# Fusion attention with each head's scores from its own 64 rows of the array, and keys without a masked product

## The reference, cut to what matters

```python
def _L0_attn_ref(x, Wq, bq, Wk, bk, Wv, bv, Wo, bo):
    # DIM 64, HEADS 4, HEAD_DIM 16, SCALE 0.25; x: (64, 205, 64)
    q = heads(x @ Wq.T + bq)
    k = heads(x @ Wk.T + bk)
    v = heads(x @ Wv.T + bv)
    attn = softmax(einsum('bhnd,bhmd->bhnm', q, k) * SCALE, axis=-1)
    out = einsum('bhnm,bhmd->bhnd', attn, v)
    out = out.transpose(0, 2, 1, 3).reshape(B, N, C)
    out = out.astype(bfloat16).astype(float32)
    return out @ Wo.T + bo

h = concatenate([image_branch(x), text_branch(x_txt)], axis=1)
h = h + _L0_attn_ref(_layernorm(h), ...)
h = h + _L0_ffn_ref(_layernorm(h), ...)
```

## Time and profile before

| what | value |
|---|---|
| median of 3 runs | 2437.77 us |
| lowest and highest run | 2432.27 and 2446.25 us |
| span of the profiled execution, first to last instruction | 2473.5 us |
| busy share of PE, PEld, DVE, ACT, POOL | 89%, 74%, 72%, 60%, 48% |
| stretch of fusion_attention | 1515.0 to 2061.5 us |
| mean granted clock of TensorE, whole span | 0.901 |
| DMA, whole span | 20.58 MB, mean 8 GB/s |

### The profile page before, as it was taken

How to read it: one execution, slowest core, us unless ns; L and a number is a source line. 1 busy time by engine, 2 the same in 40 slices (tenths; PEclk the granted TensorE clock), 3 DMA queues, 4 the chain that set the end, 5 groups by cost and what they waited for, 6 DMA issues and landing times. The chain is left out here.

```text
span 2473.5 us, 61351 instructions
## 1 busy us (share of the span) xinstructions
PE 2190.0 (89%) x19889; PEld 1822.7 (74%) x19889; DVE 1791.1 (72%) x5716; ACT 1489.8 (60%) x3226; POOL 1196.2 (48%) x1518
## 2 busy tenths in 40 slices
PE   6999999858999999999999934898888985999998
PEld 6999999746888888888888833676666764666665
DVE  5655555355888888888888845757877574888888
ACT  2222222105888888888888844656666565666663
POOL 3433333204777777777777644323433233344332
PEclk8999999957999999999999965858997576999999
DMA  2000022000000000000000000000000000000000
GB/s 87 14 20 13 13 51 43 1 1 1 2 2 3 2 3 2 2 2 2 2 2 3 2 1 1 0 0 0 0 0 0 0 0 1 8 10 8 8 10 11
DMA packets 39663, 20.58 MB, mean 8 GB/s; under 512 B 29508, under 2 KB 38852, under 8 KB 39366
## 3 DMA queue, kind: packets, MB, share of 16 engines
q1 hardware_dynamic: 39466, 18.00, 3.0%
HBM read 14.63 MB, written 3.36 MB: 7 GB/s over the span
## 5 line engine op out<-in xcount | busy, mean ns | idle before, releaser
L439 PE MATMUL im_c<-im_a_hi,im_w 128*128 128x256 f32 (+2 forms) x1920 | 427.9, 317 | 13.6 <-POOL im_a_lo L349 13.6
L439 PEld LDWEIGHTS im_c<-im_a_hi,im_w 128*128 128x128 f32 x1920 | 321.2, 191 | 30.5 <-POOL im_a_lo L349 13.8
L439 PE MATMUL im_c<-im_a_lo,im_w 128*128 128x256 f32 (+2 forms) x960 | 303.3, 316 | 0.0
L1041 POOL TENSOR_TENSOR tx_KB<-tx_KF,tx_head_rows 128x1248 fp32r<-128x1248 f32 x128 | 289.9, 2265 | 24.3 <-PE tx_scores_t L1326 15.5
L343 POOL TENSOR_TENSOR im_rstd<-im_var_eps,im_power 128x4 f32<-128x4 f32 x64 | 68.6, 1072 | 286.5 <-DVE im_var_eps L278 286.5
L902 DVE TENSOR_REDUCE tx_mpad<-tx_scores 77x8 fp32r<-77x616 f32 x256 | 202.1, 789 | 2.8 <-PE tx_maxT L1314 1.9
L1172 ACT ACTIVATE tx_PT<-tx_scores_t 77x624 f32<-77x624 f32 x256 | 175.8, 687 | 24.9 <-PE tx_scores_t L1326 18.3
L439 PEld LDWEIGHTS im_c<-im_a_lo,im_w 128*128 128x128 f32 x960 | 182.8, 190 | 8.3
L1326 PE MATMUL tx_scores_t<-tx_QP,tx_KB 128*77 128x78 f32 x2048 | 186.5, 241 | 0.0
L272 DVE BATCH_NORM_STATS2 im_stats<-im_h 128x6 f32<-128x128 f32 (+1 forms) x192 | 47.6, 302 | 190.6 <-ACT im_h L384 111.0
L1848 ACT ACTIVATE at_PT<-at_scores_t 128x824 f32<-128x824 f32 (+1 forms) x128 | 109.5, 855 | 120.9 <-PE at_scores_t L1921 120.9
(11 more groups left out here) (308 smaller groups left out, 6314.1 us busy)
## 6 DMA issues: line engine op xcount, KB each, us to landing
im_x<-x SPq DMA_DIRECT2D x16, 384.0 KB, 3.3
out<-h_img SPq DMA_DIRECT2D x32, 64.0 KB
tx_toks<-x_txt SPq DMA_DIRECT2D x1, 1925.0 KB
im_raw<-L_tok_conv_w SPq DMA_DIRECT2D x1, 1280.0 KB, 8.6
out<-h_txt SPq DMA_DIRECT2D x32, 38.5 KB
im_raw<-L_tok_conv_w SPq DMA_DIRECT2D x1, 960.0 KB, 4.8
im_raw<-L_tok_conv_w SPq DMA_DIRECT2D x1, 640.0 KB, 5.9
tx_raw_W<-L_txt_W SPq DMA_DIRECT2D x2, 256.0 KB, 7.1
```

Source lines behind the costliest of these rows:

```text
L439: last = pe.matmul(acc[:, :, d0:d1], w[c][:, slot, part], img[:, b0_:b1_, d0 + shift:d1 + shift, kj:kj + J], start=opens, stop=closes)
L1041: pool.tensor_tensor(KB[:, q % 2, t], KF[:, t].bitcast(F32).unsqueeze(1).broadcast_to([P, HPT, QW]), head_rows[:].unsqueeze(2).broadcast_t ...
```

## The change

The product with `head_rows` and with it `KB`, `head_rows` and the semaphore `k_split` are gone. `score` and `score_t` read the 64 rows of one head from `QF`, `KF` and `QP`, and so use 64 rows of the array at a time; head 0 lies on rows 0 to 63 and head 1 on rows 64 to 127. `score` has four matmuls of 206 columns for a tile instead of two of 412. The banks of `scores` and `scores_t` now belong to the head's place j instead of the tensor t, so that neighbouring matmuls write to different banks, and `find_max`, `exp` and `weigh` address them and `PT` in that order. `KF` gets a second buffer; the cut of the keys waits for the transposed scores of two samples before instead of for `k_split`.

```diff
-        lo_rows, head_rows = sb("lo_rows", [P, 2]), sb("head_rows", [P, A_HPT])
+        lo_rows = sb("lo_rows", [P, 2])
...
-        KF = sb("KF", [P, A_TENSORS, SEQP], F32R)
+        KF = sb("KF", [P, 2, A_TENSORS, SEQP], F32R)
         QF = sb("QF", [P, 2, A_TENSORS, SEQP], F32R)
-        KB = sb("KB", [P, 2, A_TENSORS, A_HPT, SEQP], F32R)
         QP = sb("QP", [P, 2, A_TENSORS, SEQP], F32R)
         mpad = sb("mpad", [P, 2, A_TENSORS, P], F32R)
-        PT = sb("PT", [P, 2, A_TENSORS, A_HPT * SEQP])
+        PT = sb("PT", [P, 2, A_HPT, A_TENSORS * SEQP])
...
-                        pool.memset(head_rows[rows, j:j + 1], 1.0).then_inc(indexed, 1)
-                        pool.wait_ge(indexed, 2 * j + 1)
                         pool.iota(row_index[rows], pattern=[[0, 1]], base=0, channel_multiplier=1).then_inc(indexed, 1)
-                        pool.wait_ge(indexed, 2 * j + 2)
...
-                    dst = QF[:, par, t] if is_q else KF[:, t]
+                    dst = QF[:, par, t] if is_q else KF[:, par, t]
                     dve.wait_ge(lo_part, m * 4 + (i + 1))
-                    if i == 0 and due(m * 2):
-                        dve.wait_ge(k_split, m * 2)
+                    if i == 0 and due(m * 2 - 2):
+                        dve.wait_ge(scored_t, m * 2 - 2)
...
-                    if live(n + 2):
-
-                        m = n + 2
-                        if due(m * 2 - 2):
-                            pool.wait_ge(scored_t, m * 2 - 2)
-                        for t in range(A_TENSORS):
-                            pool.wait_ge(qk_cut, m * 4 + (t + 1))
-                            pool.tensor_tensor(KB[:, par, t],
-                                               KF[:, t].bitcast(F32).unsqueeze(1).broadcast_to([P, A_HPT, SEQP]),
-                                               head_rows[:].unsqueeze(2).broadcast_to([P, A_HPT, SEQP]), ALU.mult)\
-                                .then_inc(k_split, 1)
...
-                        pe.wait_ge(k_split, m * 2 + 2)
                         pe.wait_ge(qk_cut, m * 4 + 4)
                     if due(m * 2 + tile):
                         pe.wait_ge(max_set, m * 2 + tile)
                     for t in range(A_TENSORS):
-                        last = pe.matmul(scores[0:n, t, 0:A_HPT * SEQP], QF[:, par, t, at:at + n],
-                                         KB[:, par, t].rearrange("p j s -> p (j s)"), start=True, stop=True)
+                        for j in range(A_HPT):
+                            head = slice(j * A_GROUP, (j + 1) * A_GROUP)
+                            last = pe.matmul(scores[0:n, j, t * SEQP:(t + 1) * SEQP], QF[head, par, t, at:at + n],
+                                             KF[head, par, t], start=True, stop=True)
...
-                            last = pe.matmul(scores_t[0:n, t, j * SEQP:(j + 1) * SEQP], KB[:, par, t, j, at:at + n],
-                                             QP[:, par, t], start=True, stop=True)
+                            head = slice(j * A_GROUP, (j + 1) * A_GROUP)
+                            last = pe.matmul(scores_t[0:n, j, t * SEQP:(t + 1) * SEQP], KF[head, par, t, at:at + n],
+                                             QP[head, par, t], start=True, stop=True)
...
-                             PT[0:kn, keys, t, j * SEQP:(j + 1) * SEQP],
+                             PT[0:kn, keys, j, t * SEQP:(t + 1) * SEQP],
```

More of the change, by code:

```diff
@@ L1654, in _ @@
                     pool.memset(oT[:].bitcast(F32), 1.0).then_inc(cleared, 1)
-                    for t in (z, mean_var, head_rows, o_rows):
+                    for t in (z, mean_var, o_rows):
                         pool.memset(t[:], 0.0).then_inc(cleared, 1)
                     pool.tensor_copy(ident_bf[:], ident[:]).then_inc(cleared, 1)
-                    pool.wait_ge(cleared, 11)
+                    pool.wait_ge(cleared, 10)
                     for j in range(A_HPT):
                         rows = slice(A_GROUP * j, A_GROUP * (j + 1))
-                        pool.memset(head_rows[rows, j:j + 1], 1.0).then_inc(indexed, 1)
-                        pool.wait_ge(indexed, 2 * j + 1)
                         pool.iota(row_index[rows], pattern=[[0, 1]], base=0, channel_multiplier=1).then_inc(indexed, 1)
-                        pool.wait_ge(indexed, 2 * j + 2)
                 @block.tensor
@@ L1677, in _ @@
                     dve.memset(outT[:], 1.0).then_inc(masks, 1)
-                    dve.wait_ge(indexed, 2 * A_HPT)
+                    dve.wait_ge(indexed, A_HPT)
                     dve.tensor_copy(row_in_group[:], row_index[:]).then_inc(masks, 1)
@@ L1711, in fusion_attention @@
             sem("x_cut"), sem("x_turned"), sem("xT_set"))
-        projected, lo_part, qk_cut, k_split, v_made, v_set = (
-            sem("projected"), sem("lo_part"), sem("qk_cut"), sem("k_split"), sem("v_made"), sem("v_set"))
+        projected, lo_part, qk_cut, v_made, v_set = (
+            sem("projected"), sem("lo_part"), sem("qk_cut"), sem("v_made"), sem("v_set"))
         scored, max_set, max_turned, q_set = sem("scored"), sem("max_set"), sem("max_turned"), sem("q_set")
@@ L1738, in find_max @@
                         dve.wait_ge(max_turned, m)
-                    dve.tensor_reduce(mpad[0:n, tile].rearrange("p t (j r) -> p t j r", r=A_GROUP)[:, :, :, 3 * A_DH],
-                                      scores[0:n, :, 0:A_HPT * SEQP].rearrange("p t (j s) -> p t j s", j=A_HPT)[:, :, :, 0:SEQ],
+                    dve.tensor_reduce(mpad[0:n, tile].rearrange("p t (j r) -> p j t r", r=A_GROUP)[:, :, :, 3 * A_DH],
+                                      scores[0:n, :, 0:A_TENSORS * SEQP].rearrange("p j (t s) -> p j t s", t=A_TENSORS)[:, :, :, 0:SEQ],
                                       AX.X, ALU.max, negate=True).then_inc(max_set, 1)
@@ L1847, in exp @@
                         act.wait_ge(weighed, m)
-                    act.activation(PT[0:n, tile], scores_t[0:n, :, 0:A_HPT * SEQP], ACT.Exp, scale=SCALE)\
+                    act.activation(PT[0:n, tile], scores_t[0:n, :, 0:A_TENSORS * SEQP], ACT.Exp, scale=SCALE)\
                         .then_inc(exped, 1)
```

## The result

The changed kernel takes 2566.73 us (median of 4 runs, 2566.2 to 2566.9) against 2442.01 us for the kernel before (4 runs, 2432.27 to 2459.76). It is slower by 125 us, 5.1% of the median before. The ratio on record is 1.062, with a 95% interval of 1.057 to 1.067, but no pair of the runs listed here goes beyond 1.055 (2566.90 over 2432.27); the text goes by the medians. The prediction had said slower, at 2469, with a range up to 2519. It had the direction, and the clock as the reason, and was wrong on the size.

What follows compares the result with a forecast made beforehand. TensorE (89% busy) and fusion_attention's cycle of waits and two-level clock were taken as the bound; 78% low clock gave 578 us for 546.5, +32 on 2473.5, less 35.7: 2469 us, range 2380 to 2519.

Steps and rivals of the forecast that it cites:

- The pairing: In score_t, two heads run side by side, four matmul slots becoming two: saves 0.22 and 0.20 us, 0.48 and 0.38 at 1.2 GHz.
- the sum: Step of fusion_attention: 7.27 - 0.42 + 0.10 = 6.95 us at 2.4 GHz, 10.32 - 0.86 + 0.20 = 9.66 at 1.2 GHz.
- The switches: TensorE drains entering or leaving the half-array form, three times each a step; price 0 to 0.34 us (0.67 at 1.2 GHz), taken 0.10.
- the late turn_x: Leaving the second score_t delays turn_x: hidden by 0.36 us of slack at 2.4 GHz, 0.10 more a step at 1.2 GHz.
- Score beside other work: `score`, run under exp and the xT copy: halving saves about 0.2 us each, twice a step, but gains nothing in step time.
- the ring: The step's cycle of waits, from score_t through exp, copy, projections, weigh and cuts to score_t: 7.27 us at 2.4 GHz.
- KB: Masked product on POOL, 128 of 0.872 us, 109.0 us in all: dropping it is worth nothing, since no critical wait depends on it.
- The clock: In fusion_attention, less matmul time in a pausing step raises 1.2 GHz time from 46% to 78%: stage 578 us, 32 more.
- The difference carried from the span to the median: Profiled span 2473.5 us lay 35.7 over the median 2437.77; this was kept, turning 2505.5 into 2469.
- No pairing: Rival, chance 0.22: in score_t the halves' loads go one after the other, only switches are paid; +9 us, 2447.
- A shorter step with the clock as before: Rival, chance 0.33: heads pair in fusion_attention without more low-clock time; -28 us (2410), or -61 (2377) at 25% low.
- a fuller PE is not what decided there: Evidence for the shorter-step case: clock low through 99 us with PE 98% busy, high through 105.8 us with 83%.

Runs made afterwards that it cites:

- the last run: Kernel before, over 128 rows, with `score` and `score_t` computing only the first head of each pair after the first sample: 2543.60 us.
- `score` alone: Changed kernel with only `score` on 64 rows a head, `score_t` reading masked keys over all 128 rows: 2592.85 us (2590.72 with the mask at zero).
- `score_t` alone: Changed kernel with only `score_t` on 64 rows a head, `score` reading masked keys over all 128 rows: 2439.29 us (2429.19 with the mask at zero).

## Why the prediction was right or wrong

- **The pairing: right.** "I take the full halving": four of score_t take 0.47 at 2.4 GHz, the figure given. With the clock held, the step is the 6.95 us of the sum. At 1.2 GHz the two score_t save 0.41 and 0.34, a little less than the 0.48 and 0.38 of the sum.
- **The switches: right in sum at 2.4 GHz, too cheap at 1.2 GHz.** The sum took 0.10 for the entry and 0.10 for the late turn_x. The first holds at 1.2 GHz: from the first load of project_v to score_t it was 0.71 and is 0.82. The second does not: project_o's weights used to load under score_t, and now their loader stands for 0.22 and then loads in the open. turn_x begins 1.26 after the second score_t where it began 1.35 after, and the xT copy 1.98 where it was 1.99, so the whole saving of the second score_t is lost. Halving alone gives 10.32 - 0.86 = 9.46 by the sum and 9.54 to 9.63 by the last run; with the form it is 9.99 to 10.03, not 9.66.
- **Score beside other work: right for the waits, the cost was elsewhere.** "Nothing is gained" holds on the ring. But this saving off the ring is what brings the low clock: 98% of the stage with `score` alone, 36% with `score_t` alone. The prediction counted both alike, in its "some 0.8 of about 6.0 busy microseconds".
- **KB: right.** 2569 with it and 2567 without. (The new wait of KF looks back two samples, not one as the prediction has it.)
- **The clock: the mechanism right in part, the share wrong.** This is the step that failed: "I take 78%, three fifths of the way". It was 96%. The share was set between 46% and 100% as if it followed the work removed in proportion. It does not: half of the removal, `score` alone, already gives 95% and more. By the prediction's own steps 96% gives 65/(0.04/6.95 + 0.96/9.66) = 618 for the stage, 40 more than 578; the step of 10.03 in the place of 9.66 makes it 641, against 638 measured. So of the 60 us over the forecast two thirds are the share, and the rest the switches at 1.2 GHz. Why it fell is also only half in the prediction: nowhere does it ask whether matmuls on 64 rows hold the clock as well as those on 128. As much matmul time taken out over 128 rows is enough for a clock of 0.51; the form is why the scores issued twice left the changed kernel at 0.53, where as many columns over 128 rows gave 0.83.
- **The difference carried from the span to the median was luck taken for a constant.** The time is the span and 1.8 us (2566.73 and 2564.9). The 35.7 were the clock: the kernel before ran at 2409 to 2466 here, the longer the lower the mean clock of the run (0.943 at 2409.24, 0.909 at 2465.62), and its profiled execution was a long one. For the same reason the 46% of low time that the forecast started from was high for this kernel; the middle one of the seven timed runs had an estimated 20%. The changed kernel, always low, lies within 0.7 us. Of the 98 us between 2469 and 2566.73, 60 are the stage and 36 are this. Without the 35.7 the forecast would have been 2505, and its upper end 2555, still short of the result.
- **The rivals.** No pairing is refuted by the rows: four of score_t take 0.47 for 0.68, and their loads 0.30 for 0.53. A shorter step with the clock as before is what `score_t` alone does (2439), but not the whole change. Its evidence, "a fuller PE is not what decided there", was sound as a reading: PE busy for 99% can go with 0.51. It did not bear the conclusion that a thinner step costs nothing.

## What to carry to other kernels

Where the granted clock of a stage moves between its two levels, a saving of matmul time is first a risk, also off the critical path: here it cost 125 us, where PE was idle for only 62 us of the stage before (546.5 less 484.6). Try the saving with the clock held, by matmuls over the whole array into a dead bank in TensorE's pauses, and count it only then; matmuls on half the rows did not serve here. And where the runs of one core spread as widely as here (49 us), the time and the mean clock of one profile are one draw out of many.

## What the runs showed of the hardware that was not expected

- The same filler columns gave 2384.82 us over 128 rows and 2682.27 over 64, with PE busy for 98% and 99% of the stage. PE's busy share does not show what holds its clock.
- Matmuls on different halves of the rows overlapped in both orders of issue that were tried: with both of head 0 issued ahead of both of head 1, four took 0.76 us, against 0.75 in alternating order and 1.16 over the whole array (1.2 GHz).
- 8 matmuls a step whose results are thrown away made the kernel before 1.0% faster (ratio 0.984 to 0.996), with a mean granted clock of 0.945 to 0.948 over the whole run where it was 0.911 to 0.943, and with the same step at 2.4 GHz (7.26 us, 7.27 before).
- In the changed kernel the clock rose to 2.4 GHz six times and fell again after 3.4 us each time. In the kernel before it held for up to 105.8 us after a rise.
